# Issuing the four loads of x together, at the head of SyncE's DMA queue, in a two-layer graph network kernel

## What is computed

```python
h = relu(layernorm(x))
x1 = swish((adj @ h) @ W0 + b0)
x = x + swish((adj @ x1) @ W0 + b0)
h = relu(layernorm(x))
a_hat = adj + eye;  d = sum(a_hat, axis=1) ** -0.5
x = x + ((a_hat * d[:, None] * d[None, :]) @ h) @ W1.T + b1
```

## Time and profile before

| | us |
|---|---|
| median of 3 runs | 1616.72 |
| lowest, highest | 1613.08, 1619.09 |
| span of the profiled execution | 1614.3 |

### The profile page before, as it was taken

One profiled execution on the slowest core, in us unless ns is written; L12 is line 12 of the kernel. 1 busy time (PEld: TensorE's weight loads), 2 busy tenths in 40 slices (PEclk: granted clock), 3 DMA queues, 4 the chain that ended last, 5 costly groups with the idle time before them and its releaser, 6 DMA issues.

```text
span 1614.3 us, 21267 instructions
## 1 busy us (share of the span) xinstructions
PE 1430.9 (89%) x6726; PEld 662.7 (41%) x6726; DVE 1144.6 (71%) x2857; ACT 660.4 (41%) x809; POOL 129.1 (8%) x94
## 2 busy tenths in 40 slices
PE   2466766789999999999997999999999999999998
PEld 1122322333444444444443444444444444444443
DVE  6998898899999998889988788888432332323331
ACT  5757667776676667576764122221100000000000
POOL 2501011000000001000000212000000000000000
PEclk9678888899999999999999999999999999999999
DMA  8478888988788878887794222111000000000000
GB/s 290 184 269 356 338 326 331 397 324 350 295 340 344 346 286 321 343 334 290 320 359 176 73 72 72 59 46 33 27 27 14 13 26 13 26 13 13 26 13 14
DMA packets 81443, 302.57 MB, mean 187 GB/s; under 512 B 5856, under 2 KB 41184, under 8 KB 48608
## 3 DMA queue, kind: packets, MB, share of 16 engines
q1 hardware_dynamic: 61168, 287.33, 45.5%
q10 hardware_dynamic: 20208, 14.42, 2.8%
HBM read 287.31 MB, written 14.42 MB: 187 GB/s over the span
## 4 chain that ended last, share of the span: by engine, by line
PE 61%; DVE 21%; DMA 12%; issue 4%; ACT 1%; DVEq 0%; SPq 0%; ACTq 0%
PE hi_ps L790 21%; PE lo_ps L791 21%; DMA ring<-adj 10%; DVE marks L1072 6%; PE job_hi_ps L725 5%; PE job_lo_ps L726 5%; PE hi_ps L750 4%; PE lo_ps L751 4%; DVE xch L1002 3%; DVE job_slot L358 2%; PE z_ps L395 2%; DMA node_b<-x 2%; DVE xch L997 1%; DVE xch L1044 1%; DVE nT L1002 1%
## 5 line engine op out<-in xcount | busy, mean ns | idle before, releaser
L897 ACT ACTIVATE unused<-ring 128x2048 uint8<-128x2048 uint32 x256 | 488.7, 1909 | 225.0 <-DMA ring<-adj 213.1
L750 PE MATMUL hi_ps<-marks,node_a 128*128 128x512 fp8e4 x1024 | 407.9, 398 | 124.3 <-DVE marks L1072 123.1
L751 PE MATMUL lo_ps<-marks,node_a 128*128 128x512 fp8e4 x1024 | 406.8, 397 | 0.0
L790 PE MATMUL hi_ps<-ring,node_a 128*128 128x512 fp8e4 x1024 | 388.1, 379 | 0.0
L791 PE MATMUL lo_ps<-ring,node_a 128*128 128x512 fp8e4 x1024 | 388.1, 379 | 0.0
L358 DVE TENSOR_SCALAR ring<-bits 128x256 uint32 (+1 forms) x784 | 168.9, 290 | 272.8 <-PE lo_ps L791 269.2
L1072 DVE TENSOR_SCALAR marks<-ring 128x2048 uint8<-128x2048 f32 x256 | 314.2, 1236 | 57.9 <-DMA ring<-adj 40.7
L725 PE MATMUL job_hi_ps<-job_slot,node_b 128*128 128x512 fp8e4 x480 | 186.7, 389 | 31.6 <-DVE job_slot L358 16.1
L750 PEld LDWEIGHTS hi_ps<-marks,node_a 128*128 128x128 f16 x1024 | 103.9, 101 | 268.7 <-issue 164.0
L790 PE MATMUL hi_ps<-ring,node_b 128*128 128x512 fp8e4 x544 | 207.2, 381 | 3.2 <-DVE ring L358 3.2
L791 PE MATMUL lo_ps<-ring,node_b 128*128 128x512 fp8e4 x544 | 207.2, 381 | 0.0
(11 more groups left out here) (117 smaller groups left out, 1047.7 us busy)
## 6 DMA issues: line engine op xcount, KB each, us to landing
ring<-adj SPq DMA_DIRECT2D x256, 1024.0 KB, 7.5
part_scratch<-xnew ACTq DMA_DIRECT2D x23, 256.0 KB, 7.3
xch<-x SPq DMA_DIRECT2D x16, 256.0 KB, 2.8
marks<-part_scratch SPq DMA_DIRECT2D x8, 512.0 KB, 4.2
xn_scratch<-xnew ACTq DMA_DIRECT2D x16, 256.0 KB, 2.3
xch<-xn_scratch SPq DMA_DIRECT2D x16, 256.0 KB, 2.9
out<-xnew ACTq DMA_DIRECT2D x16, 256.0 KB, 2.9
marks<-part_scratch SPq DMA_DIRECT2D x7, 256.0 KB, 3.0
```

Of the source, the lines that this page charges most:

```text
L750: nc.tensor.matmul(hi_ps[par][:, :], node_a16[:, j * D:(j + 1) * D], m, **ends)
L751: last = nc.tensor.matmul(lo_ps[par][:, :], node_a16[:, (NB + j) * D:(NB + j + 1) * D], m, **ends)
L790: nc.tensor.matmul(hi_ps[par][:, :], node[:, j * D:(j + 1) * D], m, **ends)
L897: nc.scalar.activation(unused[:, :], slot(i).bitcast(U32), ACT.Sign, accum_out=nz_count[:, bass.ds(c * TC + i, 1)]).then_inc(counted, 1)
```

## The change

All four parts of x are issued in a loop at the head of SyncE's list, ahead of the weights, the biases and all tiles. The issues of parts 1, 2 and 3 between the tiles of chunk 0 are gone. Sizes, semaphores, destinations and everything on the other engines stay as they are.

```diff
-            load_x(0, NORM_PARTS[0], x_in[0])
+            for part, n in enumerate(NORM_PARTS):
+                load_x(sum(NORM_PARTS[:part]), n, x_in[part])
             sp.dma_start(w_sb[:, 0:D], w0).then_inc(w_in, 16)
             sp.dma_start(w_sb[:, D:2 * D], w1t).then_inc(w_in, 16)
             sp.dma_start(b_sb[:, 0:D], b0.to_broadcast([P, D])).then_inc(w_in, 16)
...
                     for i in range(TC):
                         g = c * TC + i
-                        if first and par == 0 and i % 2 == 0 and 0 < i // 2 < len(NORM_PARTS):
-                            load_x(sum(NORM_PARTS[:i // 2]), NORM_PARTS[i // 2], x_in[i // 2])
                         if not (first and par == 0 and i < RING):
```

## The result

| | before | after |
|---|---|---|
| median of 4 runs, us | 1614.90 | 1623.49 |
| lowest, highest | 1611.38, 1619.09 | 1622.54, 1626.29 |
| span of the profiled execution | 1614.3 | 1621.2 |

The ratio is 1.0052, 95% interval 1.0032 to 1.0073. The change makes the kernel slower by some 0.2 to 0.5%; the medians differ by 8.6 us here and by 5.1 us there. Both intervals lie clear of 1, but not by much. In the later comparisons three executions of the kernel before, in a slow state, took 1762.7, 1763.5 and 3640.2 us and are left out of all ratios and medians here.

A forecast was written before the change was run, and what follows sets the result against it. TensorE takes four fifths of the time, the tile ring paces 104 to 350 us, VectorE chunk 0. Relu 1's +6.9 us shift, with nothing gained from part 3, on the 1616.7 median gave 1623.6 us, range 1615 to 1630.

The forecast's parts named there:

- The path: Chunk 0: VectorE bounds it; its 6.08 and 1.43 us waits for x go, a 12 us wait for weights comes.
- the three signs of being wrong: Square of W0 before 20 or after 26 us; norm 3's end shifted unlike relu 1; chunks 1 to 5 changing the shift.
- Transfer of x: DMA queue: parts 1, 2 and 3 take 1.7 + 3.7 + 7.0 = 12.4 us, by which everything behind lands later.
- The issue-paced rival: SyncE's loads of x: issuing paces them, up to 18.5 us, shift +13.0 us, 1629.7 us; chance 0.22, shared with other delays.
- The biases: Bias loads behind x: slowness kept and moved, so `w_in` comes at 22.8 us instead of 10.4; the largest unknown.
- both ends: Bias cost behind x: slowness kept whole, or bytes only, 0.9 us, a rival with total +2.5 us and chance 0.18.
- Two gates: Chunk 0: norm 1 waits for `w_in`, +6.1 us; ScalarE's relu 1 waits for tile 1's count, +6.9 us.
- The second wait: Norm 3: the 1.43 us wait for part 3 goes but gains nothing, as GpSimd's lock holds lines 117 and 118.
- The sum: Whole kernel: +6.9 us, from 1614.3 to 1621.2 us profiled, or 1616.7 to 1623.6 us by the median, 0.43% slower; chance 0.55.
- Carried to the end: Behind chunk 0: no later work absorbs the delay, so the +6.9 us reaches the end.
- one us later is one us at the end: Chunk 0 to the end: each us later in chunk 0 counts as one us at the end.

The follow-up runs named there:

- experiment 7: Kernel before with part 1 of x alone moved up, right behind part 0; 1613.24 us, ratio 0.9986, and 1614.08 us, 0.9986, when repeated.
- Experiment 3: Changed kernel with VectorE's wait for the weights and the square of W0 moved behind norm 1; 1622.12 us, ratio 1.0030.
- the two short kernels: Kernel before and changed kernel, each with GpSimd's low half of group 2 cut from 2048 to 16 columns; 1615.81 and 1615.95 us, one execution each.
- the second occasion: Changed kernel and kernel before run again without an edit; 1622.38 us in 12 runs against 1617.24 in 29, ratio 1.0023.
- the three kernels whose chunk 0 ends sooner: Kernel before with part 1 alone moved up (0.9986 twice), every part one pair of tiles sooner (1.0008, 0.9988), or part 1 up and biases behind part 2 (0.9982).
- experiment 9: Kernel before with 72 more block statistics on VectorE ahead of norm 3; 1633.01 us, ratio 1.0105.
- experiment 4: Changed kernel with the two bias loads issued behind tile 3 on a semaphore of their own; 1619.43 us, ratio 1.0012.
- experiment 8: Kernel before with every part of x one pair of tiles sooner; 1616.74 us, ratio 1.0008, and 1614.53 us, 0.9988, when repeated.

## Why the prediction was right, and where it was off

**The path.** Right: chunk 0 is VectorE's and its loads'; the two waits for x vanish, a wait for the weights takes the place of the first, and chunk 0 ends later. None of the three signs of being wrong came: the square of W0 is at 20.77, inside 20 to 26, norm 3's end has relu 1's shift (4.46 and 4.52), and chunks 1 to 5 neither took the shift back nor added to it clearly (3.7 to 4.9 us by VectorE's marks).

**Transfer of x.** 12.4 us by landings of the old order; measured 17.7 less 5.15, where part 0 landed, 12.55. The issue-paced rival (up to 18.5 us) is refuted: part 3 landed 7.2 us behind part 2, where its transfer took 7.0 before. SyncE was in fact held in issuing, 7.13 us in the load of W0, but x was still moving then (DMA share 1.05 from 10 to 17 us, in the last section), so no transfer time was lost. That the queue was full is my reading.

**The biases, the term that was too large.** I moved their slowness unchanged and put `w_in` at 22.8; it came at 20.75. The time from x to the second bias was 3.0 us and not 5.45. Therefore norm 1's shift was +3.9 instead of +6.1, tile 0 landed at 23.2 instead of 25.2, and relu 1's shift was +4.5 instead of +6.9. I had both ends, 0.9 us and 5.45, and the truth was near the middle. In experiment 7 the second bias landed at 4.12 + 6.0 = 10.1, no later than before although part 1 stood ahead of it: a part of the slow loads runs beside the tail of x. That is how I read it; no run takes it apart.

**Two gates.** Right in kind: ScalarE's count of tile 1 shifts more than norm 1, and it is this shift that norm 3's end has (4.52 and 4.46). Experiment 3 bears it out: 10 us taken off norm 1 are worth 0.9. The prediction left out how relu 1's shift gets into norm 2, which is VectorE's own work and would by itself have come 6.1 us later, not 6.9 (3.8, not 4.5, by the trace). It is GpSimd's group 1, which follows relu 1 and holds line 117 of norm 2.

**The second wait worth nothing.** Right, by the two short kernels, and for the reason given. The Trainium skill (SBUF — State Buffer, section "SBUF: two separate sides") calls the shared port pair an exclusive lock held for the whole instruction; the trace agrees, with 2.87 us for an operation of 0.24 us that ends 0.08 us after GpSimd's.

**The sum.** 6.9 us was forecast, 6.9 us lie between the spans, and that agreement is partly luck: the terms of chunk 0 were 2.4 us too large, and 2.4 us came later, in a stretch in which two executions of one kernel differ by up to 4.8. That 1623.6 us meets 1623.49 is luck as well: it was 6.9 us on a median of 1616.7, and with one more run that median was 1614.90, so the step between the medians is 8.6 us, and 5.1 us on the second occasion. What the traces show the change to do in chunk 0 is about 4.5 us, 1.003.

**Carried to the end.** Nothing took the delay back, neither 4.5 nor 10.5 us of it, and the times of the three kernels whose chunk 0 ends sooner followed their gains, one occasion excepted. That nothing is added later isn't shown, and "one us later is one us at the end" stays open on that side: experiment 9 lost 6.7 us more there, a part of it in an idle time that I can't explain, and both traces of the changed kernel lost 2.5 and 3.7 us behind chunk 12.

## What to carry to other kernels

Where one queue feeds several readers, a load that moves forward pushes back everything it passes: list what it passes and who waits for that, small loads with a shared semaphore among them. Here they hid under the first piece of work and cost nothing until they stood behind 4 MB. Move forward only what its reader waits for, so far that the wait is covered (part 1 here) and no further. Ahead of counting a removed wait as a gain, look at what the freed engine meets next: the wait for part 3 was removed in front of an engine that held the next operation, and was worth nothing.

## What the runs showed of the hardware beyond what I had expected

- Two loads of 64 KB that copy one row of 512 bytes to all partitions took 2.7 us of the queue behind x (experiment 4), about as long as a tile of 1 MB (2.5 us from tile 0 to tile 1).
- The loads of x, whose rows are 512 bytes, moved at 288 GB/s (305 before the change), the tiles, with 8 KB in one piece per partition, at 426. The last column of two stretches of the changed kernel:

```profile
10.00:17.00 7.00, 0.00 (x0) 0.00 (x0) 0.86 (x6) 3.18 (x8) 2.59 (x2) 1.00 1.05 288
...
22.00:26.00 4.00, 0.00 (x0) 0.00 (x0) 3.42 (x21) 2.31 (x3) 0.00 (x0) 1.00 1.01 426
```

- Block statistics are listed with 0.28 us each but follow each other every 0.195 us, and GpSimd's instructions don't slow them: 32 of them took 6.28 us in experiment 8 while GpSimd worked from 38.39 to 46.43, and 6.27 in experiment 9 with GpSimd idle.
- GpSimd's instructions hold VectorE's short operations of every norm that they meet: 0.17 us became up to 1.97 in norm 1 (experiment 7) and up to 1.99 in norm 2 (experiment 3), and 0.24 became 2.87 in norm 3. Each started while a GpSimd instruction ran and ended with it, within 0.1 us.
- From the end of norm 3 to the end of the first pass, two executions of one kernel differed by up to 4.8 us of 831. What moves them isn't known; it isn't the mean granted clock (0.92 to 0.93 in all).
